# A GeGLU kernel's first microseconds: the first weight transfer is issued without a wait for GpSimd's constants, and one filler product is taken out behind the scale products

## The reference

```
scale = cond @ norm_w.T + 1.0
ms = jnp.mean(x * x, axis=-1, keepdims=True)
h = x * (scale[:, None, :] * jax.lax.rsqrt(ms + EPS))
u = h @ up_w.T
val, gate = jnp.split(u, 2, axis=-1)
h = val * jax.nn.gelu(gate, approximate=False)
hq = h + jax.lax.stop_gradient(act_quant(h) - h)
wq = down_w + jax.lax.stop_gradient(weight_quant(down_w) - down_w)
y = hq @ wq.T
return y + x
```

## Time and profile before

| | |
|---|---|
| time, median of 3 runs | 425.6 us (425.3 to 425.83) |
| the profiled execution | 425.47 us, of which the span of the program is 423.7 us |
| TensorE busy | 420.1 us (99%) |
| VectorE, ScalarE, GpSimd busy | 283.1, 186.8, 168.6 us |

### The profile page before, as it was taken

How to read it: one execution, slowest core, us unless ns; L and a number is a source line. 1 busy time by engine, 2 the same in 40 slices (tenths; PEclk the granted TensorE clock), 3 DMA queues, 4 the chain that set the end, 5 groups by cost and what they waited for, 6 DMA issues and landing times.

```text
span 423.7 us, 7696 instructions
## 1 busy us (share of the span) xinstructions
PE 420.1 (99%) x2087; PEld 339.5 (80%) x2087; DVE 283.1 (67%) x540; ACT 186.8 (44%) x335; POOL 168.6 (40%) x323
## 2 busy tenths in 40 slices
PE   9999999999999999999999999999999999999997
PEld 6888878888888888888887788887888888888786
DVE  4895775747756577665767657576574775657676
ACT  6764443535435244443534525444353543525441
POOL 2543542534425343353424525254252442534320
PEclk9999999999999999999999999999999999999999
DMA  8634342542335433352433435334254232543324
GB/s 268 211 57 108 113 99 74 149 99 74 99 78 148 96 95 88 93 145 75 112 92 112 104 74 148 85 89 99 74 149 99 74 99 74 148 99 91 82 51 125
DMA packets 82520, 45.01 MB, mean 106 GB/s; under 512 B 68560, under 2 KB 69328, under 8 KB 82384
## 3 DMA queue, kind: packets, MB, share of 16 engines
q1 hardware_dynamic: 82080, 44.47, 40.5%
q10 hardware_dynamic: 432, 0.46, 0.3%
HBM read 20.00 MB, written 8.39 MB: 67 GB/s over the span
## 4 chain that ended last, share of the span: by engine, by line
PE 99%; DVE 0%; issue 0%; DVEq 0%
PE p_gate L796 41%; PE p_val L796 41%; PE p_y L816 13%; PE p_y L706 1%; PE p_gate L721 0%; DVE y_sb L546 0%; PE p_val L780 0%; PE p_val L775 0%; PE p_gate L780 0%; PE p_gate L775 0%; PE p_val L733 0%; PE p_val L721 0%; PE p_gate L733 0%; PE p_gate L727 0%; PE p_val L774 0%; PE p_gate L774 0%
## 5 line engine op out<-in xcount | busy, mean ns | idle before, releaser
L650 DVE SCALAR_TENSOR_TENSOR h<-p_val,rstd,gelu 128x512 f32<-128x512 f32 x124 | 92.5, 746 | 118.0 <-PE p_val L796 117.0
L442 ACT ACTIVATE gelu<-p_gate,rstd 128x512 f32<-128x512 f32 x124 | 85.0, 685 | 140.0 <-PE p_gate L796 132.6
L388 ACT ACTIVATE q<-q_rounded 128x1024 bf16<-128x1024 f32 x63 | 66.6, 1058 | 83.4 <-DVE q_rounded L607 83.4
L314 POOL TENSOR_TENSOR mean_sq_eps<-mean_sq,rms_eps 128x1 f32<-128x1 f32 x64 | 12.3, 192 | 228.6 <-ACT squares L376 228.6
L796 PE MATMUL p_gate<-up_hi,a_lo 128*128 128x512 f32 x248 | 79.2, 400 | 0.0
L796 PE MATMUL p_val<-up_hi,a_hi 128*128 128x512 f32 x248 | 77.9, 395 | 0.0
L796 PE MATMUL p_val<-up_hi,a_lo 128*128 128x512 f32 x248 | 77.9, 395 | 0.0
L796 PE MATMUL p_gate<-up_lo,a_hi 128*128 128x512 f32 x248 | 77.9, 395 | 0.0
L796 PE MATMUL p_val<-up_lo,a_hi 128*128 128x512 f32 x248 | 77.9, 395 | 0.0
L796 PE MATMUL p_gate<-up_hi,a_hi 128*128 128x512 f32 x248 | 77.9, 395 | 0.0
L593 DVE TENSOR_REDUCE h_max<-h 128x1 f32<-128x1024 f32 x63 | 76.7, 1218 | 1.7
(11 more groups left out here) (87 smaller groups left out, 251.0 us busy)
## 6 DMA issues: line engine op xcount, KB each, us to landing
xt_in<-x_t SPq DMA_DIRECT2D x32, 256.0 KB, 2.8
x_all<-x SPq DMA_DIRECT2D x32, 256.0 KB, 2.9
out<-y_sb SPq DMA_DIRECT2D x30, 256.0 KB, 2.2
up_raw<-up_w_t SPq DMA_DIRECT2D x7, 256.0 KB, 5.4
down_raw<-down_w_t SPq DMA_DIRECT2D x1, 1024.0 KB, 8.0
q_t<-q SPq DMA_TRANSPOSE x63, 3.1
up_raw<-up_w_t ACTq DMA_DIRECT2D x1, 256.0 KB, 2.9
out<-y_sb SPq DMA_DIRECT2D x2, 128.0 KB, 1.8
```

What stands on the lines that cost most here:

```text
L314: pool.tensor_tensor(mean_sq_eps[:, j:j + 1], mean_sq[:, j:j + 1], rms_eps[:, :], ALU.add).then_inc(pool_step, 1)
L388: act.activation(q[j % 2][:, :], q_rounded[j % 2][:, :], ACT.Copy, bias=-ROUND).then_inc(q_ready, 1)
L442: act.activation(gelu[c][:, :], p_gate[c][:, :], ACT.Gelu, scale=rstd[:, j:j + 1]).then_inc(gelu_done, 1)
L650: nc.vector.scalar_tensor_tensor(h[s][:, c * W:(c + 1) * W], p_val[c][:, :], rstd[:, j:j + 1], gelu[c][:, :], op0=ALU.mult, op1=ALU.mult). ...
```

## The change

ScalarE's wait for `consts_ready` ahead of its first transfer is removed, and the second row of fillers on TensorE has five products and not six.

```
@@ -402,7 +402,6 @@
                 act.activation(gelu[t][:, :], p_gate[t][:, :], ACT.Gelu,
                                scale=rstd[:, t:t + 1]).then_inc(gelu_done, 1)
 
-            act.wait_ge(consts_ready, 1)
             act.dma_start(up_raw[:, 0, 0, :], up_w_t[0, 0, :, 0, :]).then_inc(up_in[0], 16)
             act.preload_act_table(ACT.Gelu)
             high_part(0, 0)
@@ -711,7 +710,7 @@
                 rows = slice(k * C, (k + 1) * C)
                 nc.tensor.matmul(scale_bank[k][:, 0:B], cond_norm_sb[rows, B:B + P], cond_norm_sb[rows, 0:B],
                                  start=True, stop=True).then_inc(scale_done, 1)
-            keep_busy(6)
+            keep_busy(5)
 
             def first_product(t, which, k):
                 bank = (p_gate, p_val)[which][t]
```

## The result

The changed kernel takes 427.14 us, the median of 22 runs (425.44 to 428.12), against 425.5 us before in 22 runs (425.26 to 425.94): 1.6 us more. By the ratio that goes with the comparison, which follows the mean and not the median, it is 1.0029 (95% interval 1.0022 to 1.0037), or 1.2 us. The forecast, 425.5 in a range of 425.1 to 426.0, was wrong. A median alone hides what the list of runs shows: 7 of the 22 lie at 425.44 to 425.86, as before, and 14 above 426.5. The medians of these two groups are 425.49 and 427.34. So the same program sometimes loses nothing and mostly loses 1.4 to 2.6 us. (One run of the kernel before in the later comparisons took 848.52 us; it is left out of all that follows.)

The account below looks back on a forecast made before the run. TensorE's fixed train of matmuls was taken as the bound. ScalarE's wait 0, filler at most -0.21, limited by the second weight slice to -0.10: 425.47 to 425.37 us, 425.5 as a median, range 425.1 to 426.0.

Parts of the forecast that it names:

- What bounds the kernel: TensorE's fixed train of matmuls from about 6 us; the change moves only its start or its first microseconds' pace.
- ScalarE's issue at 0.75: Without its wait, ScalarE issues the first weight transfer 0.23 us earlier, at 0.75; this gains 0 by itself.
- The shift d: How much earlier the transfers behind the first weights, x and the second weight slice, land: 0.06 to 0.23 us.
- the upper bound, 0.2: Most that the start's later transfers could shift: the whole 0.23 us by which ScalarE issues earlier.
- my 0.10: Value in us taken for the earlier landing of the start's later transfers, nearer the lower end of 0.06 to 0.23.
- The filler: One filler less behind the scale products lets the first real product start earlier: 0.12 to 0.21 us in front.
- the recorded 0.12: Gain in us in front if the clock rises at 5.9 regardless: the third product begins at 6.0, not 6.12.
- the limit: TensorE's gain in front is kept only as far as the second weight slice lands earlier: 0.10 us.
- The scale inputs: Rival at the start: cond_norm loses its head start, landing at 3.56 at worst; 0 to +0.3 us, chance 0.12.
- the 289 GB/s of the sum: Transfer rate assumed at the start: 262 KB of weights ahead of cond_norm take 0.91 us.
- The clock: Rival at the start: the rise comes at 9.3, not 5.9, eight slow products, +1.5 us; chance 0.05 with other losses.
- the rival's 427.1: Time in us forecast if the clock stays low at the start, +1.5; chance 0.05 with other losses beyond 0.85.

Follow-up runs that it names:

- e9: Kernel before with 2 fillers and not 6 behind the scale products (13 ahead, ScalarE's wait kept): 426.78 us.
- e5: Kernel before with 9 fillers ahead of the scale products and 4 behind (13 and 6 before), wait kept: 427.01 us.
- e2: Kernel before with five fillers and not six behind the scale products, ScalarE's wait kept: 425.52 us, ratio 1.0004.
- e1: Kernel before with ScalarE's wait removed and six fillers kept: 427.18 us, ratio 1.0025.
- e11: Changed kernel with ScalarE's first transfer cut in two, a quarter of the columns (64 KB) first: 425.88 us.
- e10: Changed kernel again without an edit, for a second profile and more runs: 427.11 us, the profiled run 425.57.
- e12: Changed kernel a third time without an edit, for a profile alone: 425.62 us.
- e3: Changed kernel with 17 fillers and not 13 ahead of the scale products: 425.96 us, ratio 1.0006.
- e4: Kernel before with SP's first two transfers swapped, so that cond_norm comes behind x: 427.2 us, ratio 1.0029.
- e6: Kernel before with 9 fillers ahead of the scale products and 8 behind (13 and 6 before), wait kept: 426.94 us.
- e8: Kernel before with ScalarE issuing nothing at the start; SP issues cond_norm, first weights, x and the rest in one queue: 426.64 us.

## Why the prediction was wrong

**What bounds the kernel: right.** Nothing behind 17 us changed, and the whole difference lies in the start and the pace of the train.

**ScalarE's issue at 0.75: right** (0.74), and the table load stayed covered.

**The shift d: wrong in one half.** The second slice landed 3.8 us after its issue at 1.69, at 5.5 and not 5.7: the upper bound, 0.2, rather than my 0.10. x and the first weights landed later, by 0.1 and 0.3. I had counted only idle time to be filled, and no price for a slow start of the transfers, as in the stretches at 128 and 136 GB/s. That two queues starting together are its cause isn't shown: e9, with ScalarE's issue 0.23 us behind, moved 44 and 99 GB/s in the same stretches.

**The filler: right to be worth little, for a reason not forecast.** The sum had a_hi ready at about 5.00 and up to 0.21 to win in front. In e5 and e9, where nothing stands before it, the first real product waits for a_hi until 5.19 and 5.23, so no more than 0.10 to 0.14 could be won; e2 shows 0.12. That this equals the recorded 0.12 is chance, since that figure was for the third product with the rise at 5.9: in e2 the third product came 0.08 later than before and not 0.12 earlier. I took the limit to be the second slice; in e2 it was the clock.

**The scale inputs: the cover was priced too high.** "The worst is that all 256 KB of weights go ahead of it", landing at 3.56. It landed at 4.34, 4.44 and 4.25 (issue plus time to landing) in three of five profiles with equal starts, and at 3.8 in the other two. In all five the transfers went at well under the 289 GB/s of the sum up to about 3 us. The late scale inputs were priced at 0.3 at most; in the profile the first real product alone is 0.52 late. The Trainium skill (DMA: Bandwidth & Descriptors, Queues, rings and completion order) says that an engine takes a whole packet of descriptors from one queue before it turns to another. The profiles of the changed kernel and of e1 agree with the direction, with 0.15 and 0.14 MB of weights moved by 3.0 us against 0.03 MB of cond_norm, and so does e11. In e10, e12 and e3 both queues advanced side by side, and cond_norm was late all the same. A delay of 1.7 us for 0.9 us of weights the rule does not explain.

**The clock: the failed step.** "real products take the filler's place without a gap, so TensorE is as busy as before" was the step on which the whole forecast rested, and it holds only behind the scale products; ahead of them TensorE stood still for 0.67 us. I held the late scale inputs and the late clock to be two rivals, priced at +0.3 and +1.5, with chances of 0.12 and 0.05. They are one chain. cond_norm late makes the pause, and a pause ahead of the rise makes the clock late. e5 shows the second link without late inputs, e1 and e4 with all the fillers, and e3 closes the pause and with it the loss. The eight slow products at 0.19 were sized rightly: 1.6 us of the profile's 2.13, with 0.52 of late start beside them. That the rival's 427.1 meets the measured 427.14 is luck: that median mixes two groups, the larger of which lies at 427.34. The rival's condition, a "longer pause about the scale products", was named and not followed back to what would lengthen it, and the signs listed for being wrong (cond_norm beyond 3.4, products spaced at 0.43 past 6 us) are the two that came.

**The pause that was already there.** I took the stretch from 3.50 to 4.22 as a pause and as evidence that pauses are harmless. It was none to speak of: the scale products begin at 3.64 and fill it. Between that and 0.41 us of plain idleness (e9) lies the difference between 1 run in 116 above 426.5 and 7 in 12.

The Trainium skill (TensorE: Matmul & The Clock Gate, Part 1) says that the moment of the rise, and with it the number of products at the low level, differs from run to run of one kernel. The traces agree: by 4.26, at about 6.2 and at about 9.9 in three profiles of the changed kernel. The pauses of these three differ as well (0.55, 0.17 and 0.67 us), so not all of that spread is the run's own; 3.6 to 6.2 without a pause is.

**What stays open.** Why the transfers move so little for a microsecond in the profiles with equal starts and in e9; why cond_norm took 1.9 to 2.7 us in kernels with the same issues (e2, e5, e6, e9 and before); whether e6's pause or its fewer fillers cost it; and what the runs that weren't profiled looked like inside.

## What to carry to other kernels

A filler is there to leave no pause before the clock has risen; behind the rise, pauses of 1.2 us left the level up (e8, e11). Before removing a wait or a filler at the start, ask which small transfer the next work on TensorE needs, and what may now get in front of it. A wait that seems pointless (for GpSimd's constants, which ScalarE never reads here) may be what gives a small, urgent transfer 0.23 us of head start over a large one: the profiles with it had cond_norm after 1.9 to 2.7 us, those without after 3.1 to 3.7. And when a change sits in the clock's first microseconds, take many runs and look at their spread: one profile can show either group.

## What was not expected of the hardware

Two transfers issued at the same moment by SP and ScalarE took 3.1 to 3.7 us (80 KB) and 3.4 to 3.7 us (256 KB) in five profiles, where 0.23 us between them gave 1.9 to 2.7 and 2.9 to 3.1 in five others: the large one got longer too, not only the small one. With a pause of 0.4 to 0.8 us in TensorE's first 5.2 us, before the clock had risen, the 2.4 GHz level came between 7.8 and 9.9 us in six profiles, where it came between 3.6 and 6.2 in the five without one; the unlucky runs of the changed kernel lose 1.4 to 2.6 us. A pause of 1.2 us behind the rise left the level up. And one and the same program, the changed kernel, falls in two groups that lie 1.8 us apart with one run of 22 between.
